# A post-norm attention and FFN block on one core: attention rows turned and normalised in the attention stage instead of the FFN stage

## The chip, the cores and the metric

The kernel runs on one core of a Trainium2 chip. The metric is the device time of one launch in microseconds (us), the median of several runs. TensorE (PE) multiplies into PSUM, which has eight banks of 512 fp32 columns; VectorE (DVE), ScalarE (ACT) and GpSimd (POOL) do the rest; SyncE (SP) only issues DMAs. Each engine runs its own instruction stream in order and waits on semaphores.

## The reference

The inputs are x of 4 x 2048 x 512 in fp32, four 512 x 512 weight matrices, a scale and a bias. There are 16 heads of 32 columns.

```python
q, k, v = x @ Wq.T, x @ Wk.T, x @ Wv.T           # split into 16 heads of 32
attn = softmax(q @ k.T / sqrt(32), axis=keys)
x = layernorm(x + attn @ v)                       # heads side by side: 512 columns
w = (weights >= 0) * 2 - 1
y = clip((x @ w.T) * scale + bias, -100, 100)
out = layernorm(x + y)
```

## The kernel before

Three stages follow one another, each a block of its own in which all engines start and end together.

**Projection** (`project`) makes q, k and v for 16 blocks of 512 tokens. Its products are full-array matmuls of 128 rows x 128 columns (L228). Once in each block, between two of them, stand eight matmuls that use 32 columns of the array each and four of which run side by side (L250).

**Attention** (`attend`) goes through 16 items (4 sequences x 4 groups of 4 heads), each with four query blocks of 512 queries (`qb`; 64 blocks in all, numbered `st`), each with 16 key tiles `kt` of 128 keys. For one key tile and two heads (a unit, two a tile) PE makes scores (L637, 8 matmuls, 32 array columns each, four side by side) into one of three PSUM slots; ACT takes the exponential of all 1024 columns of the unit (L780) into `probs`, a ring of eight tiles; PE multiplies them with v (L669, also on 32 array columns) into a bank that holds the block's output, with channels on the partitions and queries on the columns. PE's scores run `LAG` = 2 key tiles ahead of its values. A score unit waits for the exponential of three units earlier, the values of a tile for both exponentials of the tile.

The softmax denominators are sums over all keys. DVE adds `probs` of neighbouring tiles in five groups (`EDGES`) into `total` and `partial`; POOL issues DMAs that add the `partial` groups onto `total`. When block `st` is past, the work that is left of it is done between the key tiles of block `st`+1:

- DVE copies the block's output from its bank to SBUF after tile 2 (`copy_out`, L809), and SP stores it to DRAM, channel-major.
- PE sums `total` over its partitions with a matrix of ones (`denominators`, L690), 128 queries at a time, behind tiles 8, 10, 12 and 13 (`DEN_TILES`), again on 32 array columns a head. The denominators stand replicated over the 32 channels of a head.
- DVE copies them after tile 13 (`copy_den`, L814), and SP stores one row for each head.

**Normalise and FFN** (`normalise_and_ffn`) goes through 64 tiles of 128 tokens. It is a software pipeline written out by hand: in step `j` each engine does its part for tiles that entered at different times (`ATTN, LN1, TRANS, FFN, CLIP, LN2 = 0, 1, 2, 4, 5, 6` steps back). In one step:

- PE: four transposes of the attention tile into token-major order (L1003) and one of the denominators (L1004); four transposes of the first layernorm's result y (L1010); the bias row (L1017) and twelve matmuls of the FFN (L1021).
- DVE: clip (L1108), statistics of the two layernorms (L1084), reciprocal of the denominators (L1115), aggregation (L1089), the product of attention and reciprocal (L1122), reciprocal deviations (L1094), offsets (L1098), the low half of y's transposes (L1132).
- ACT: two square roots (L1035), the high half of y's transposes (L1055), the first layernorm's result y (L1039), then the second's.
- POOL: the two residual additions (L978, L985). SP loads attention, denominators and x for four tiles at a time.

Of the kernel before, what the change touches and what calls it, by code (L numbers as in the profile page):

```python
# [26 lines left out]
P = 128  # L27
# [30 lines left out]
DEN_TILES = (8, 10, 12, 13)  # L58
DEN_EDGES = (0, 128, 256, 384, BLK)
OUT_AFTER = 2  # L60
DEN_AFTER = 13
# [345 lines left out]
def attend(nc, ctx, dram, banks, ffn, first, early):  # L407
# [18 lines left out]
    ones = sb("ones", [P, HD], FP32)  # L426
# [7 lines left out]
    out_sb, den_sb = wf_scaled[:, 0:2, :], wf_scaled[:, 2:4, :]  # L434
# [11 lines left out]
    a_out = sem("a_out")  # L446
    a_dout = sem("a_dout")
    a_store = [sem(f"a_store{h}") for h in range(2)]
# [15 lines left out]
    HEAD = DEN_TILES[-1] + 1  # L464
# [8 lines left out]
    def out_bank(qb):  # L473

        return 2 * SLOTS + qb % 2
# [8 lines left out]
    def _(sp):  # L484
        def store(it, qb):

            cols = slice(qb * BLK, (qb + 1) * BLK)
            sp.wait_ge(a_out, it * QB + qb + 1)
            dst = dram["attn"].rearrange("n (g p) t -> (n g) p t", p=P)[bass.ds(it, 1), :, cols]
            sp.dma_start(dst.rearrange("o p t -> (o p) t"), out_sb[:, qb % 2, :]).then_inc(a_store[qb % 2], 16)  # L490
            sp.wait_ge(a_dout, it * QB + qb + 1 + 2)
            dst = dram["den"].rearrange("(i h) t -> i h t", h=G)[bass.ds(it, 1), :, cols]
            sp.dma_start(dst.rearrange("o h t -> (o h) t"), den_sb[0:P:HD, qb % 2, :]).then_inc(a_store[qb % 2], 16)

        def finish_stores():
            for h in range(2):
                sp.wait_ge(a_store[h], (LAST * QB // 2) * 32 + 32)
            attn_first, den_first, first_in = first
            sp.dma_start(attn_first[:], dram["attn"][0, :, 0:BLK].rearrange("(c p) t -> p c t", p=P)).then_inc(first_in, 16)
            sp.wait_ge(a_const, 5)  # L500
            sp.dma_start(den_first[0:H, :], dram["den"][0:H, 0:BLK]).then_inc(first_in, 16)
# [82 lines left out]
        for h in range(2):  # L584
            sp.wait_ge(a_store[h], ITEMS * QB // 2 * 32 + 32)

    @block.gpsimd
    def _(pool):
        nc.gpsimd.memset(ones[:], 1.0).then_inc(a_const, 1)  # L589
# [5 lines left out]
        nc.gpsimd.memset(first[1][:], 0.0).then_inc(a_const, 4)  # L595
# [23 lines left out]
    def _(pe):  # L619
# [53 lines left out]

        def denominators(it, qb, piece):
            st = it * QB + qb
            cols = slice(DEN_EDGES[piece], DEN_EDGES[piece + 1])
            split = it is LAST and qb == QB - 1
            parts = [total[:, qb % 2], partial[:, GROUPS - 2]] if split else [total[:, qb % 2]]
            if piece == 0:
                for pair in range(2):  # L680
                    if split:
                        pe.wait_ge(a_merge[qb % 2][pair], merged_after(it, qb, MERGES - 1))
                        pe.wait_ge(a_sum[pair], (st + 1) * KT + P_RING)
                    else:
                        pe.wait_ge(a_merge[qb % 2][pair], merged_after(it, qb, MERGES))
                pe.wait_ge(a_out, st + 1)
            for part in parts:
                for h in range(G):
                    rows = slice(HD * h, HD * h + HD)
                    last = nc.tensor.matmul(banks[rows, out_bank(qb), cols], ones[:], part[:, h, cols],  # L690
                                            start=(part is parts[0]), stop=(part is parts[-1]))
            last.then_inc(a_den, 1)

        def steps(scores, it, phase, qb, tiles):

            for kt in tiles:
# [8 lines left out]

                if kt in DEN_TILES and qb > 0:
                    denominators(it, qb - 1, DEN_TILES.index(kt))
                elif kt in DEN_TILES and not (isinstance(it, int) and it == 0):
                    denominators(it - 1, QB - 1, DEN_TILES.index(kt))

        def item(scores, it, phase):
# [6 lines left out]
            else:  # L718
                for piece in range(len(DEN_TILES)):
                    denominators(it, QB - 1, piece)  # L720

# [14 lines left out]
        with pe.If(needed < 1):  # L736
            pe.wait_ge(a_const, 1)
# [3 lines left out]
        with pe.Else():  # L741
            pe.wait_ge(a_const, 1)
# [22 lines left out]

# [21 lines left out]
    def _(dve):  # L787
        for pair in range(2):
            dve.sem_inc(a_sum[pair], P_RING)
        dve.sem_inc(a_store[0], 32)  # L790
        dve.sem_inc(a_store[1], 32)
# [14 lines left out]
        def copy_out(st, parity):  # L806
            dve.wait_ge(a_pv, st * KT + KT + P_RING)
            dve.wait_ge(a_store[parity], (st - parity) * 16 + 32)
            nc.vector.tensor_copy(out_sb[:, parity, :], banks[:, out_bank(parity), :]).then_inc(a_out, 1)  # L809

        def copy_den(st, parity):
            dve.wait_ge(a_den, (st + 1 + 2) * len(DEN_TILES))
            dve.wait_ge(a_store[parity], (st - parity) * 16 + 32)
            nc.vector.tensor_copy(den_sb[:, parity, :], banks[:, out_bank(parity), :]).then_inc(a_dout, 1)  # L814

        def item(it, first):
            for qb in range(QB):
                st = it * QB + qb
                for kt in range(KT):
                    if kt in EDGES:  # L820
                        continue
# [14 lines left out]
                    if kt == OUT_AFTER and not (first and qb == 0):  # L836
                        copy_out(st - 1, (qb - 1) % 2)
                    if kt == DEN_AFTER and not (first and qb == 0):
                        copy_den(st - 1, (qb - 1) % 2)
# [3 lines left out]
        copy_out(ITEMS * QB - 1, 1)  # L843
        copy_den(ITEMS * QB - 1, 1)


def normalise_and_ffn(nc, ctx, dram, x, ffn, first, banks, out):
# [16 lines left out]
    attnT = [first[0], sb("attnT1", [P, DC, BLK], FP32)]  # L864
    den_in = [first[1], sb("den_in1", [P, BLK], FP32)]
    rden = sb("rden", [P, 2, H], FP32)
    attn = sb("attn", [P, 2, D], FP32)
# [15 lines left out]
    f_den = sem("f_den")  # L883
    f_in = [first[2], sem("f_in1")]
    f_x = [sem(f"f_x{k}") for k in range(2)]
    f_aT = sem("f_aT")
    f_rden = sem("f_rden")
    f_attn = sem("f_attn")
# [12 lines left out]

    def aT_bank(s):
        return banks[:, s % 2, :]

    def den_bank(s):
        return banks[:, 6 + s % 2, 0:H]
# [32 lines left out]
    def _(sp):  # L939
# [3 lines left out]
        def load(b, batch, column, k):  # L943

            sp.wait_ge(f_res[0], b * TPB + TPB)
            src = dram["attn"][bass.ds(batch, 1), :, bass.ds(column, BLK)]
            sp.dma_start(attnT[k][:], src.rearrange("o (c p) t -> p (o c) t", p=P)).then_inc(f_in[k], 16)
            src = dram["den"].rearrange("(n h) t -> n h t", n=N)[bass.ds(batch, 1), :, bass.ds(column, BLK)]
            sp.dma_start(den_in[k][0:H, :], src.rearrange("o h t -> (o h) t")).then_inc(f_in[k], 16)
# [3 lines left out]
        sp.wait_ge(f_den, 1)  # L953
# [9 lines left out]
    def _(pool):  # L963
        nc.gpsimd.memset(ident3[:], 0.0).then_inc(f_const, 1)
        nc.gpsimd.memset(eps[:], EPS).then_inc(f_const, 1)
        nc.gpsimd.memset(den_in[1][:], 0.0).then_inc(f_den, 1)
# [6 lines left out]
        def step(r, j):  # L973
# [6 lines left out]
            if t is not None:  # L980
                if s % TPB == 0:
                    pool.wait_ge(f_x[s // TPB], r * 16 + 16)
                pool.wait_ge(f_attn, t + 1 + 2)
                pool.wait_ge(f_y[0], t + 1)
                nc.gpsimd.tensor_tensor(res1[:, s % 2], attn[:, s % 2], x_in[:, s // TPB, s % TPB], ALU.add).then_inc(f_res[0], 1)  # L985
# [4 lines left out]
    def _(pe):  # L990
# [3 lines left out]
        def step(r, j):  # L994
            t, s = tile(r, j, ATTN)
            if t is not None:
                k = s // TPB
                cols = slice(s % TPB * P, (s % TPB + 1) * P)
                if s % TPB == 0:
                    pe.wait_ge(f_in[k], r * 32 + 32)  # L1000
                pe.wait_ge(f_attn, t + 1)
# [71 lines left out]
    def _(dve):  # L1073
        dve.sem_inc(f_attn, 2)
# [26 lines left out]
        def step(r, j):  # L1101
# [9 lines left out]
            attn_t, attn_s = tile(r, j, ATTN)  # L1111
            if attn_t is not None:
# [117 lines left out]
```

## Time and profile before

| | us |
|---|---|
| median of 3 runs (2723.27 to 2724.31) | 2723.47 |
| the profiled execution, its own time | 2722.63 |
| its span from the first to the last instruction | 2720.5 |
| projection, until the first scores | about 560 |
| attention | about 1878 |
| normalise and FFN | about 282 |

The rows of the trace give for each engine when an instruction or a run of like instructions starts and how long it is busy. A PE matmul's duration includes its way through the array, so rows of neighbouring matmuls overlap: the work that one puts on PE is the distance between starts. A busy share of 100% on PE therefore doesn't say that PE has no time left.

### The profile page before, as it was taken

What the parts mean: (1) busy time and instruction counts of PE and PEld (TensorE: products, weight loads), DVE (VectorE), ACT (ScalarE), POOL (GpSimd) and SP (SyncE); (2) the same over time, 40 slices, a digit from 0 to 9 for tenths busy, and PEclk for the clock granted to TensorE, in tenths of its full rate; (3) what the DMA queues carried; (4) which work ended last, traced back from release to release, by engine and by line L of the source; (5) the groups of instructions that cost most, each with busy time, mean ns of one, the idle gap of its engine ahead of it and who ended that gap; (6) DMA issues with size and microseconds to landing.
All of it is one profiled execution on the core that took longest, in us unless ns stands there. A gap on an engine that the chain in (4) does not pass through costs nothing.

```text
span 2720.5 us, 92280 instructions
## 1 busy us (share of the span) xinstructions
PE 2685.3 (99%) x38720; PEld 1581.4 (58%) x38720; DVE 2193.1 (81%) x2623; ACT 2260.5 (83%) x2726; POOL 615.2 (23%) x661
## 2 busy tenths in 40 slices
PE   9999999999999999999999999999999999979998
PEld 8888888744454444444444444445455544447887
DVE  7444444379989989989989989989998998978998
ACT  5333333399999999999999999999999999965665
POOL 1000000012222222222222222222222222225665
PEclk9999999999999999999999999999999999989999
DMA  6555555589898999989899898999989899975553
GB/s 230 191 195 193 186 186 186 197 170 199 172 208 176 200 188 193 202 168 210 172 199 194 179 207 175 199 184 199 194 173 206 177 201 187 184 178 176 190 189 136
DMA packets 262711, 513.33 MB, mean 189 GB/s; under 512 B 20674, under 2 KB 135362, under 8 KB 260164
## 3 DMA queue, kind: packets, MB, share of 16 engines
q0 software_dynamic: 73440, 267.42, 52.4%
q1 hardware_dynamic: 179108, 222.61, 25.4%
q10 hardware_dynamic: 9792, 17.83, 1.7%
q8 instruction: 297, 4.87, 0.7%
q14 instruction: 74, 0.61, 0.1%
HBM read 122.43 MB, written 117.96 MB: 88 GB/s over the span
## 4 chain that ended last, share of the span: by engine, by line
PE 97%; DVE 1%; ACT 1%; issue 1%; DMA 0%; SPq 0%; POOL 0%; ACTq 0%; POOLq 0%; DVEq 0%
PE banks L637 34%; PE banks L669 33%; PE banks L228 19%; PE banks L1021 7%; PE banks L690 2%; PE banks L1010 1%; PE banks L1003 1%; PE banks L1017 1%; PE banks L250 0%; PE banks L1004 0%; PE banks L256 0%; DMA scratch_v<-v_out 0%; DMA score_rows<-scratch_k_lo 0%; ACT y L1039 0%; DVE qk_raw L357 0%
## 5 line engine op out<-in xcount | busy, mean ns | idle before, releaser
L780 ACT ACTIVATE probs<-banks 128x1024 f32<-128x1024 f32 x2048 | 1877.5, 1781 | 4.1 <-PE banks L637 4.1
L637 PE MATMUL banks<-score_rows 97*32 97x512 f16 x16384 | 1259.4, 382 | 4.9 <-POOL den_in L595 3.9
L669 PE MATMUL banks<-probs,v_keys 128*32 128x256 f32 x16384 | 1251.6, 379 | 0.5 <-ACT probs L780 0.5
L609 POOL DMA_DIRECT2D total<-partial x510 | 439.0, 861 | 1439.2 <-DVE partial L835 498.6
L835 DVE TENSOR_TENSOR partial<-partial,probs 128x1024 f32<-128x1024 f32 x640 | 748.4, 1221 | 0.0
L669 PEld LDWEIGHTS banks<-probs,v_keys 128*32 128x32 f32 x16384 | 510.5, 110 | 405.8 <-ACT probs L780 0.9
L831 DVE TENSOR_TENSOR partial<-probs 128x1024 f32<-128x1024 f32 x512 | 604.2, 1222 | 119.9 <-issue 109.7
L637 PEld LDWEIGHTS banks<-score_rows 97*32 97x32 f16 x16384 | 351.4, 95 | 509.7 <-ACT probs L780 413.2
L356 DVE TENSOR_TENSOR qk_lo<-banks,qk_hi 128x512 f16<-128x512 f32 x128 | 88.4, 691 | 241.7 <-ACT qk_hi L311 241.6
L311 ACT ACTIVATE qk_hi<-banks 128x512 f16<-128x512 f32 x128 | 76.0, 594 | 185.2 <-PE banks L228 185.2
L228 PE MATMUL banks<-xT_hi,w_hi 128*128 128x512 f32 x512 | 197.6, 390 | 0.0
L228 PE MATMUL banks<-xT_lo,w_hi 128*128 128x512 f32 x512 | 197.5, 389 | 0.0
L228 PE MATMUL banks<-xT_hi,w_lo 128*128 128x512 f32 x512 | 197.4, 389 | 0.0
L831 DVE TENSOR_TENSOR total<-probs 128x1024 f32<-128x1024 f32 x128 | 150.9, 1222 | 6.7 <-ACT probs L780 6.3
L835 DVE TENSOR_TENSOR total<-total,probs 128x1024 f32<-128x1024 f32 x128 | 151.0, 1223 | 0.0
L315 ACT ACTIVATE v_out<-banks 128x512 f32<-128x512 f32 x64 | 38.2, 597 | 123.9 <-PE banks L228 123.8
L589 POOL MEMSET ones<- 128x32 f32 x1 | 0.1, 124 | 501.4 <-POOLq L1190 501.4
L1035 ACT ACTIVATE std<-mean_var,eps 128x1 f32<-128x1 f32 x128 | 31.8, 289 | 97.8 <-DVE mean_var L1089 97.5
L228 PEld LDWEIGHTS banks<-xT_hi,w_lo 128*128 128x128 f32 x512 | 96.2, 188 | 19.9
L228 PEld LDWEIGHTS banks<-xT_lo,w_hi 128*128 128x128 f32 x512 | 96.2, 188 | 19.9
L228 PEld LDWEIGHTS banks<-xT_hi,w_hi 128*128 128x128 f32 x512 | 96.1, 188 | 19.8
L690 PE MATMUL banks<-total,ones 128*32 128x128 f32 x2048 | 101.8, 273 | 4.4 <-DVE wf_scaled L809 3.7
(95 smaller groups left out, 2180.4 us busy)
## 6 DMA issues: line engine op xcount, KB each, us to landing
total<-partial POOLq DMA_DIRECT2D x510, 512.0 KB, 6.2
scratch_q_raw<-qk_raw SPq DMA_DIRECT2D x16, 1024.0 KB, 5.7
scratch_k_raw<-qk_raw SPq DMA_DIRECT2D x16, 1024.0 KB, 5.7
scratch_v<-v_out SPq DMA_DIRECT2D x16, 1024.0 KB, 5.1
score_rows<-scratch_q_hi SPq DMA_DIRECT2D x128, 128.0 KB, 5.5
score_rows<-scratch_k_hi SPq DMA_DIRECT2D x128, 128.0 KB, 4.3
v_keys<-scratch_v SPq DMA_DIRECT2D x64, 256.0 KB, 7.0
scratch_attn<-wf_scaled SPq DMA_DIRECT2D x64, 256.0 KB
```

The costliest lines, as they stand in the source:

```text
L228: last = nc.tensor.matmul(bank(j), *parts[i], start=(c == 0 and i == 0), stop=(c == DC - 1 and i == 2))
L311: nc.scalar.activation(qk_hi[:, j, :], bank(j), ACT.Copy).then_inc(s_hi, 1)
L315: nc.scalar.activation(v_out[:, j - NQK, :], bank(j), ACT.Copy).then_inc(s_hi, 1)
L356: nc.vector.tensor_tensor(qk_lo[:, j, :], bank(j), qk_hi[:, j, :], ALU.subtract).then_inc(s_lo, 1)
L609: pool.dma_start(total[:, qb % 2, heads], partial[:, g - 1, heads], accum_op=ALU.add).then_inc(a_merge[qb % 2][pair], 16)
L637: last = nc.tensor.matmul(scores_of(phase, unit)[part, i, :], k_rows[:, h, keys], q_rows[:, h, qb * BLK:(qb + 1) * BLK], start=True, stop= ...
L669: last = nc.tensor.matmul(banks[rows, out_bank(qb), cols], v_keys[:, kt, rows], probs[:, kt % P_RING, h, cols], start=(kt == 0 and part == ...
L690: last = nc.tensor.matmul(banks[rows, out_bank(qb), cols], ones[:], part[:, h, cols], start=(part is parts[0]), stop=(part is parts[-1]))
L780: nc.scalar.activation(probs[:, kt % P_RING, heads, :], scores_of(it % SLOTS, qb * UNITS + u), ACT.Exp, scale=SCALE / GAIN ** 2).then_inc( ...
L831: nc.vector.tensor_tensor(into, probs[:, (kt - 1) % P_RING, heads], probs[:, kt % P_RING, heads], ALU.add).then_inc(a_sum[pair], 2)
L835: nc.vector.tensor_tensor(into, into, probs[:, kt % P_RING, heads], ALU.add).then_inc(a_sum[pair], 1)
L1021: last = nc.tensor.matmul(ffn_bank(s), part[:, s % 4, cols], w[:, c, :], start=False, stop=(c == DC - 1 and w is wf_lo))
```

## The change

The output of a query block and its denominators are now transposed on PE inside the next query block, divided there by DVE, and stored as normalised rows, token-major: `scratch_attn` becomes 4 sequences x 4 head groups x 2048 tokens x 128 channels. The FFN stage loads these rows and adds x to them; its five transposes a tile of L1003 and L1004, its reciprocal L1115 and its product L1122 are gone. Behind the key tiles of block `st`+1 there is now:

- after tile 2, DVE `copy_out` as before, into one buffer instead of two;
- behind tile 4, PE `turn_output`: four transposes of 128 x 128, the whole array, into the bank from which the output was just copied; after tile 5, DVE `copy_turned` to SBUF;
- behind tiles 8, 9, 10 and 11 the denominators, with `select` (a column of ones, a different one for each 128 queries) in the place of `ones`, so that the four pieces add up in the same 128 columns;
- at tile 12, DVE `copy_den` of these 128 columns; behind tile 13, PE `turn_denominators`, one transpose; after tile 14, DVE `invert_den` (16 values a partition); at tile 15, DVE `normalise` (512 columns, SBUF to SBUF).

SP waits for `a_norm` and issues one store of 256 KB a block in rows of 512 bytes, in the place of one of 2 KB rows and one of the denominators. In the FFN stage the attention rows of four tiles come in four DMAs.

```diff
-DEN_TILES = (8, 10, 12, 13)
+DEN_TILES = (8, 9, 10, 11)
+TURN_TILE = 4
+DEN_TURN_TILE = 13
+OUT_AFTER, TURNED_AFTER, DEN_AFTER, INVERT_AFTER, NORMAL_AFTER = 2, 5, 12, 14, 15
...
+        def turn_output(it, qb):
+            st = it * QB + qb
+            pe.wait_ge(a_out, st + 1)
+            for c in range(TPB):
+                cols = slice(c * P, (c + 1) * P)
+                last = nc.tensor.transpose(banks[:, out_bank(qb), cols], out_sb[:, cols], ident2[:])
+            last.then_inc(a_turn, 1)
...
-                pe.wait_ge(a_out, st + 1)
+                pe.wait_ge(a_turned, st + 1)
...
-                    last = nc.tensor.matmul(banks[rows, out_bank(qb), cols], ones[:], part[:, h, cols],
+                    last = nc.tensor.matmul(banks[rows, out_bank(qb), 0:P], select[:, piece, :], part[:, h, cols],
...
+        def turn_denominators(it, qb):
+            pe.wait_ge(a_dcopy, it * QB + qb + 1)
+            nc.tensor.transpose(banks[:, out_bank(qb), P:2 * P], den_sb[:], ident2[:]).then_inc(a_dturn, 1)
...
+        def copy_turned(st, parity):
+            dve.wait_ge(a_turn, st + 1)
+            dve.wait_ge(a_norm, st)
+            nc.vector.tensor_copy(turned, banks[:, out_bank(parity), :]).then_inc(a_turned, 1)
...
+        def invert_den(st, parity):
+            dve.wait_ge(a_dturn, st + 1)
...
+        def normalise(st, parity):
+            dve.wait_ge(a_dout, st + 1 + 2)
...
 def normalise_and_ffn(nc, ctx, dram, x, ffn, first, banks, out):
...
-                for c in range(DC):
-                    nc.tensor.transpose(aT_bank(s)[:, c * P:(c + 1) * P], attnT[k][:, c, cols], ident3[:])
-                nc.tensor.transpose(banks[:, 6 + s % 2, 0:P], den_in[k][:, cols], ident3[:]).then_inc(f_aT, 1)
...
-                nc.vector.reciprocal(rden[:, attn_s % 2], den_bank(attn_s)).then_inc(f_rden, 1)
...
-                nc.vector.tensor_tensor(attn[:, attn_s % 2].rearrange("p (h d) -> p h d", h=H),
-                                        aT_bank(attn_s).rearrange("p (h d) -> p h d", h=H),
-                                        rden[:, attn_s % 2].unsqueeze(2).to_broadcast([P, H, HD]), ALU.mult).then_inc(f_attn, 1)
```

PE in one query block of attention, before, from the last values of key tile 8 to the first of tile 10 (`probs,v_keys` are values, `score_rows` scores, `total,ones` denominators; 32x marks the array columns used):

```order
L669 MATMUL banks<-probs,v_keys 32x256 x4
L690 MATMUL banks<-total,ones 32x128 x4
L637 MATMUL banks<-score_rows 32x512 x8
L669 MATMUL banks<-probs,v_keys 32x256 x4
L637 MATMUL banks<-score_rows 32x512 x8
L669 MATMUL banks<-probs,v_keys 32x256 x4
L637 MATMUL banks<-score_rows 32x512 x8
L669 MATMUL banks<-probs,v_keys 32x256 x4
```

PE in the same block now, around tile 4, and then around tile 13 (`ident,wf_scaled` are the transposes of the output, `ident,den_sb` that of the denominators; 128x is the whole array):

```order
L642 MATMUL banks<-score_rows 32x512 x8
L674 MATMUL banks<-probs,v_keys 32x256 x4
L685 MATMUL banks<-ident,wf_scaled 128x128 x4
L642 MATMUL banks<-score_rows 32x512 x8
L674 MATMUL banks<-probs,v_keys 32x256 x4
```

```order
L642 MATMUL banks<-score_rows 32x512 x8
L674 MATMUL banks<-probs,v_keys 32x256 x4
L713 MATMUL banks<-ident,den_sb 128x128
L642 MATMUL banks<-score_rows 32x512 x8
L674 MATMUL banks<-probs,v_keys 32x256 x4
```

Before, every matmul of the attention stage stood on 32 array columns; now two places in each block have the whole array between them.

PE in one step of the FFN stage before, from the last FFN matmul of the step ahead:

```order
L1021 MATMUL banks<-wf_lo,yT_hi 128x512
L1003 MATMUL banks<-ident,attnT 128x128 x4
L1004 MATMUL banks<-ident,den_in 128x128
L1010 MATMUL banks<-ident,y 128x128 x4
L1017 MATMUL banks<-bias_rows,bias_ones 128x512
L1021 MATMUL banks<-wf_hi,yT_hi 128x512
```

The same place now:

```order
L1063 MATMUL banks<-wf_lo,yT_hi 128x512
L1052 MATMUL banks<-ident,y 128x128 x4
L1059 MATMUL banks<-bias_rows,bias_ones 128x512
L1063 MATMUL banks<-wf_hi,yT_hi 128x512
```

The transposes of y now follow directly on the FFN matmuls of the step ahead.

## Rows read from the trace of the kernel before

**Rows 1.** The page, its first line

```profile
span 2720.5 us, 92280 instructions
```

**Rows 2.** Groups by line: busy us, mean ns of one, idle before

```profile
L780 ACT ACTIVATE probs<-banks 128x1024 f32<-128x1024 f32 x2048 | 1877.5, 1781 | 4.1 <-PE banks L637 4.1
```

**Rows 3.** Windows: each engine's busy us, granted PE clock, DMA share, GB/s

```profile
1000.00:1500.00 500.00, 500.00 (x9276) 240.30 (x9272) 452.52 (x411) 500.00 (x547) 116.73 (x136) 1.00 0.93 192
...
2600.00:2650.00 50.00, 50.00 (x274) 41.95 (x273) 48.29 (x154) 31.04 (x64) 31.98 (x26) 1.00 0.58 196
```

**Rows 4.** Timeline of PE in attention: start us, busy us, engine, line

```profile
1213.40 0.39 PE L690 MATMUL banks<-total,ones 128*32 128x128 f32 x8
1213.61 0.61 PE L637 MATMUL banks<-score_rows 97*32 97x512 f16 x8
...
1214.48 0.61 PE L637 MATMUL banks<-score_rows 97*32 97x512 f16 x8
...
1229.02 0.61 PE L637 MATMUL banks<-score_rows 97*32 97x512 f16 x8
...
1229.94 0.61 PE L637 MATMUL banks<-score_rows 97*32 97x512 f16 x8
```

**Rows 5.** Waits over the whole run: us in total, times, longest

```profile
PEld banks L637 <- ACT probs L780: 413.2, 1410, 0.8
```

**Rows 6.** Timeline of PE in the projection, where the array is divided

```profile
101.57 0.39 PE L228 MATMUL banks<-w_hi,xT_lo 128*128 128x512 f32 x1
101.89 0.61 PE L250 MATMUL banks<-squares,head_sum 128*32 128x512 bf16 x8
102.43 0.50 PE L228 MATMUL banks<-w_hi,xT_hi 128*128 128x512 f32 x1
102.77 0.39 PE L228 MATMUL banks<-w_lo,xT_hi 128*128 128x512 f32 x1
```

**Rows 7.** Timeline of PE in one FFN step

```profile
2602.18 0.60 PE L1003 MATMUL banks<-ident,attnT 128*128 128x128 f32 x4
...
2602.72 0.60 PE L1010 MATMUL banks<-ident,y 128*128 128x128 f32 x4
...
2603.08 0.48 PE L1017 MATMUL banks<-bias_rows,bias_ones 128*128 128x512 f32 x1
...
2605.96 0.40 PE L1021 MATMUL banks<-wf_lo,yT_hi 128*128 128x512 f32 x1
...
2606.20 0.60 PE L1003 MATMUL banks<-ident,attnT 128*128 128x128 f32 x4
```

**Rows 8.** Timeline of DVE and ACT in the same FFN step

```profile
2602.47 0.69 DVE L1108 TENSOR_SCALAR clipped<-banks 128x512 f32<-128x512 f32 x1 [0.23 <-PE banks L1021]
...
2603.07 1.27 DVE L1084 BATCH_NORM_STATS2 stats<-res 128x6 f32<-128x512 f32 x2
...
2604.27 0.24 DVE L1115 RECIPROCAL rden<-banks 128x16 f32<-128x16 f32 x1
...
2604.43 0.26 DVE L1089 BATCH_NORM_AGGREGATE mean_var<-stats 128x2 f32<-128x6 f32 x2
...
2604.58 0.48 ACT L1035 ACTIVATE std<-mean_var,eps 128x1 f32<-128x1 f32 x2 [1.51 <-DVE mean_var L1089]
2604.63 0.69 DVE L1122 TENSOR_TENSOR attn<-banks,rden 128x512 f32<-128x512 f32 x1
...
2604.97 0.58 ACT L1055 ACTIVATE yT_hi<-banks 128x512 fp32r<-128x512 f32 x1
...
2605.68 1.52 ACT L1039 ACTIVATE y<-res,offset,rstd 128x512 f32<-128x512 f32 x2
```

**Rows 9.** Timeline of DVE in attention, the denominators' copy

```profile
1223.19 0.69 DVE L814 COPY wf_scaled<-banks 128x512 f32<-128x512 f32 x1 [0.94 <-PE banks L690]
```

**Rows 10.** Timeline from the end of attention into the FFN stage

```profile
2434.66 0.69 DVE L814 COPY wf_scaled<-banks 128x512 f32<-128x512 f32 x1 [2.97 <-PE banks L690]
...
2438.27 0.39 SPq L941 DMA_DIRECT2D x_res<-in_x  x1
```

More of the change, by code:

```diff
@@ L485, in store @@
         def store(it, qb):
[L487 to L493, printed above, removed]
+            sp.wait_ge(a_norm, it * QB + qb + 1)
+            dst = dram["attn"].rearrange("n g (b c q) f -> (n g) b q c f", b=QB, q=P)[bass.ds(it, 1), qb]
+            src = normal[:, qb % 2, :].rearrange("q (c f) -> q c f", c=TPB)
+            sp.dma_start(dst.rearrange("o q c f -> (o q) c f"), src).then_inc(a_store[qb % 2], 16)
         def finish_stores():
             for h in range(2):
[L497 to L501, printed above, removed]
+                sp.wait_ge(a_store[h], (LAST * QB // 2) * 16 + 16)
+            attn_first, first_in = first
+            for t in range(TPB):
+                src = dram["attn"][0, :, t * P:(t + 1) * P, :].rearrange("g p f -> p g f")
+                sp.dma_start(attn_first[:, t].rearrange("p (g f) -> p g f", g=NG), src).then_inc(first_in, 16)
         sp.wait_ge(early.s_vst, 16 * NBLK)
@@ L689, in denominators, with behind @@
                     rows = slice(HD * h, HD * h + HD)
-                    last = nc.tensor.matmul(banks[rows, out_bank(qb), cols], ones[:], part[:, h, cols],
-                                            start=(part is parts[0]), stop=(part is parts[-1]))
+                    last = nc.tensor.matmul(banks[rows, out_bank(qb), 0:P], select[:, piece, :], part[:, h, cols],
+                                            start=(piece == 0 and part is parts[0]),
+                                            stop=(piece == TPB - 1 and part is parts[-1]), skip_group_check=True)
             last.then_inc(a_den, 1)
+        def turn_denominators(it, qb):
+            pe.wait_ge(a_dcopy, it * QB + qb + 1)
+            nc.tensor.transpose(banks[:, out_bank(qb), P:2 * P], den_sb[:], ident2[:]).then_inc(a_dturn, 1)
+        def behind(it, qb, kt):
+            if kt == TURN_TILE:
+                turn_output(it, qb)
+            if kt in DEN_TILES:
+                denominators(it, qb, DEN_TILES.index(kt))
+            if kt == DEN_TURN_TILE:
+                turn_denominators(it, qb)
         def steps(scores, it, phase, qb, tiles):
@@ L704, in steps @@
                     values(it, qb, kt, half)
[L706 to L709, printed above, removed]
+                if qb > 0:
+                    behind(it, qb - 1, kt)
+                elif kt < HEAD and not (isinstance(it, int) and it == 0):
+                    behind(it - 1, QB - 1, kt)
         def item(scores, it, phase):
@@ L718, in item @@
             else:
-                for piece in range(len(DEN_TILES)):
+                turn_output(it, QB - 1)
+                for piece in range(TPB):
                     denominators(it, QB - 1, piece)
+                turn_denominators(it, QB - 1)
         def all_items(scores):
@@ L818, in item, with finish_last @@
                 st = it * QB + qb
+                def finish_last(kt):
+                    if first and qb == 0:
+                        return
+                    if kt == OUT_AFTER:
+                        copy_out(st - 1, (qb - 1) % 2)
+                    if kt == TURNED_AFTER:
+                        copy_turned(st - 1, (qb - 1) % 2)
+                    if kt == DEN_AFTER:
+                        copy_den(st - 1, (qb - 1) % 2)
+                    if kt == INVERT_AFTER:
+                        invert_den(st - 1, (qb - 1) % 2)
+                    if kt == NORMAL_AFTER:
+                        normalise(st - 1, (qb - 1) % 2)
                 for kt in range(KT):
                     if kt in EDGES:
+                        finish_last(kt)
                         continue
@@ L835, in item @@
                             nc.vector.tensor_tensor(into, into, probs[:, kt % P_RING, heads], ALU.add).then_inc(a_sum[pair], 1)
[L836 to L839, printed above, removed]
+                    finish_last(kt)
         for it in range(ITEMS):
```

103 lines of the change are left out of this document (45 added, 58 removed).

## The prediction, made before the changed kernel ran

> **What bounds the kernel now.** The time divides at the stage borders, and each stage has its own limit, so I read the windows of one stage first and then the timeline inside it. In attention (the window from 1000) [rows 3] PE and ACT both show 500 of 500 us, DVE 452.5. Which of the two sets the pace is told by the other views. ACT takes 1877.5 us for 2048 units, 0.917 us each [rows 2], with next to no idle time. PE's busy share hides waits: its weight loads waited 1410 times for ACT, 413 us in total [rows 5], and the starts of score groups come in two rhythms [rows 4]: 0.92 us when PE waits for ACT (1229.02 to 1229.94) and 0.87 us when it catches up after a denominators' piece (1213.61 to 1214.48). So ACT is the bound of attention, 32 x 0.917 = 29.34 us a query block, and PE follows closely. How closely is the number on which the case turns.
>
> PE's own demand: from 1213.61 to 1229.02 lie 17 units and three pieces of denominators of 0.21 us each (1213.40 to 1213.61 is one) [rows 4]. (15.41 - 0.64) / 17 = 0.869 us a unit. A block needs 32 x 0.869 + 4 x 0.21 = 28.65 us. **PE has 0.69 us to spare in each block of 29.34.**
>
> In the FFN stage the reader is to see a period of 4.02 us a tile on PE, from one group of L1003 to the next, without a gap [rows 7], and DVE with 48.29 of 50 us just beneath it [rows 3].
>
> **What the FFN stage loses.** The five transposes take 2602.72 - 2602.18 = 0.54 us [rows 7], 0.107 each; what is left of the step is 4.02 - 0.54 = 3.48. If PE stayed the bound, 64 tiles would give 34 us. It doesn't stay: with the attention transposes gone, PE's first work in a step is the transposes of y, and y comes late. I follow the loop. DVE's clip starts 0.20 to 0.29 us after PE's last matmul has streamed (2602.18 to 2602.47 is the 0.29). From the clip to the start of y on ACT lie 2605.68 - 2602.47 = 3.21 us [rows 8]. Of these the reciprocal took 0.16 (2604.27 to 2604.43); the 0.61 of L1122 lay beside ACT's square roots and isn't won, since the second aggregation still has to wait for its statistics and ACT has roots and yT_hi ahead of y. I take 3.03 (bounds 2.92 and 3.05), and y takes 0.81, so y is there 3.84 us after the clip. PE then needs 0.04 us of handing over and 3.48 of work until the clip after the next can start, 0.24 later. y of step j is transposed in step j+1, so this loop spans two steps: (3.84 + 0.04 + 3.48 + 0.24) / 2 = 3.80 us a step. Before, the 0.54 us of L1003 and L1004 stood at the head of the step and covered this wait. DVE's and ACT's own round (clip 0.6, statistics 1.2, aggregation to yT_hi about 0.65, yT_hi 0.58, yT_lo 0.6) comes to some 3.65 us, under it. Gain: 0.22 us x 64 tiles = **-14 us**, bounds -8 and -34. The four loads of attention rows instead of two are hidden: a block of four tiles lasts 15 us.
>
> **What the attention stage gets, PE.** The same five transposes, 0.54 us a block. The denominators cost what they did: 4 pieces x 16 matmul records, only earlier. To the 0.54 comes what no row of attention shows: these are the only matmuls there on the whole array. The nearest rows are in the projection, where eight matmuls on 32 columns stand between full ones [rows 6]. From the last full matmul before (101.57) to the second after (102.77) pass 1.20 us. The work in it is 0.23 + 0.43 + 0.23 = 0.89 (full matmuls follow one another at 0.23; eight of 512 columns side by side in fours take 0.43, as a score group does). **0.31 us is lost for one excursion**, at both edges together: the array runs empty, and the next weights aren't loaded beneath the running matmuls (the weights of L228 start with its matmul). The rows show the reverse nesting, narrow inside wide, but both have one edge of each kind. A block now has two excursions, at tiles 4 and 13: 0.62 us. PE's demand is 28.65 + 0.54 + 0.62 = 29.81, against ACT's 29.34. PE becomes the bound by 0.47 us a block, in 63 blocks 30 us, less the head start of some 1 us that the three slots hold: **+29 us**. Bounds: 0 if the excursions are hidden (29.19 stays under 29.34); +41 if each costs 0.40, which is what the fp32 weight loads add if none overlaps.
>
> The Trainium skill, TensorEngine Tiling (Array Packing), section Tiling Modes, has the rule for this: changing the tiling mode, not merely the tile, drains TensorE. The trace agrees in that the 0.31 us stands only where the number of active columns changes. It gives no price; by the rule with a free drain the stage would stay at ACT's pace, which is the third rival below.
>
> **DVE in attention.** Before 0.69 x 2 for the copies; now 0.69 x 2 (output and its transposes), 0.69 for the product (as L1122 [rows 8]), 0.24 for the reciprocal (as L1115) and about 0.3 for 128 columns: 2.6 us, 1.2 more a block. DVE is busy 452.5 of 500 us, 26.55 of 29.34 [rows 3], and 0.94 us of its idle time is the wait for the last denominators between two additions of the last group [rows 9]; the new place of this copy, between two groups, lies in slack. 27.8 of 29.3 fits, and fits better if PE stretches the block. PE's new waits queue scores behind them: for `copy_out` at tile 4, where DVE is some 2 us ahead, for `copy_turned` at tile 8 and for `copy_den` at tile 13, both further ahead. ACT has no instruction more; POOL's merges are untouched. SP waits up to four units longer in `store`; behind it stand loads of q and v for the next item, needed more than 10 us later. The store of 256 KB has four times the packets on DMA engines that are busy 0.93 [rows 3]; nothing waits for it.
>
> **The border of the stages.** After the last block the chain is longer by the transposes, two copies for one, a transpose and reciprocal, the product: 0.4 + 0.7 + 0.1 + 0.25 + 0.7, less 0.4 for the smaller copy, and five handovers of 0.2 to 0.3. That delays the last store by 3 to 5 us; the store of 2.9 us behind it (2435.35 to 2438.27 [rows 10]) and x's load follow as before. **+4 us.**
>
> **Sum.** The profiled execution took 2722.63 us, with a span of 2720.5 [rows 1], 0.8 us under the median of 2723.47. 2722.6 + 29 - 14 + 4 = 2741.6 us.
>
> **The rivals.**
> 1. The forecast: PE bounds attention, y's loop bounds the FFN stage; 2741.6, own range 2729 to 2752.
> 2. PE stays the bound of the FFN stage (y is ready earlier than I think, by 0.6 us): 34 us gained, 2722.6 + 29 - 33 + 4 = 2723, no change. For it: the busy sum of no other engine is over 3.2 us a step. Against: the order of ACT's queue.
> 3. The excursions are hidden or cheap, and attention stays at ACT's pace; faster. Threshold: 0.075 us an excursion, (0.69 - 0.54) / 2. 2722.6 - 14 + 4 = 2713, with rival 2 on top 2694. For it: PE's weight loads wait for ACT 0.29 us at a time (413.2 / 1410 [rows 5]), so the price might fall into waits. Against: the waits add up to 0.69 us a block only, and 0.54 is already spent on the transposes.
> 4. DVE or the DMAs bind too: late copies make PE wait at tiles 4 or 13 with scores queued behind, 0.2 us or more a block; 2753 and up.
>
> **How the numbers follow.** Chances: forecast 0.53, rival 2 0.15, rival 3 0.22, rival 4 0.10. A measurement here tells about 0.2%, 5.4 us, from no change. Slower: forecast and rival 4, 0.62 or a little more; same: rival 2 and the costlier side of rival 3, 0.17; faster: 0.20. The range leaves out half of rival 4 and the lower end of rival 3: 2706 to 2752.
>
> **What the profile after would show.** In attention, PE's weight loads of scores hardly wait for ACT any more, ACT gets idle time in small pieces of 0.47 us a block in all, and blocks last 29.8 us; around the transposes, starts are 0.1 us wider than the work. In the FFN stage, PE waits for y each second step or in each, with steps of 3.8 us. Wrong would be a block of 29.34 with PE still waiting (rival 3), a step of 3.48 (rival 2), or PE waiting for DVE in attention (rival 4).

## The result, and the profile after

The changed kernel takes 2738.98 us, median of 5 runs (2738.05 to 2739.43), against 2723.27 before: a ratio of 1.0058 with a 95% interval of 1.0045 to 1.0072, so 15.7 us slower. 2741.6 was predicted. The profiled execution has a span of 2736.6 us, 16.1 more than [rows 1].

The page and the waits of the kernel after, the lines that answer to [rows 2] and [rows 5]:

```profile
span 2736.6 us, 92216 instructions
...
L812 ACT ACTIVATE probs<-banks 128x1024 f32<-128x1024 f32 x2048 | 1896.7, 1073 | 11.7 <-PE banks L642 5.4
```

```profile
PEld banks L713 <- issue: 25.9, 63, 0.4
PEld banks L685 <- issue: 25.9, 63, 0.4
PEld banks L642 <- ACT probs L812: 17.4, 83, 0.4
```

PE's weight loads of scores used to wait 413.2 us for the exponentials, 1410 times; now it is 17.4 us, 83 times. (Weight loads run ahead of the matmuls, so these waits are no measure of PE's spare time: 413.2 us would be 6.5 us a block, and PE had 0.69.) PE has nothing left to wait for: it has become the bound of the attention stage. The other two lines are the first weight load of each whole-array place. The weight loads pause there for 0.41 us, 63 times each: these weights are not loaded beneath the matmuls ahead. ACT doesn't show its new idle time as such. Before, a record lasted 1781 ns at a distance of 917 from one start to the next, so neighbours overlapped by 0.86 us; now it is 1073 ns at 930, and they overlap by 0.14. The busy sum is even larger than before. The reader should take the bound from who waits, not from the busy sums.

The timeline of PE around the two whole-array places of one block (start us, busy us, engine, line), kernel after, which answers to [rows 4] and [rows 6]:

```profile
1202.38 0.65 PE L642 MATMUL banks<-score_rows 97*32 97x512 f16 x8
1202.82 0.65 PE L674 MATMUL banks<-probs,v_keys 128*32 128x256 f32 x8
1203.40 0.33 PE L713 MATMUL banks<-ident,den_sb 128*128 128x128 f32 x1
1203.66 0.62 PE L642 MATMUL banks<-score_rows 97*32 97x512 f16 x8
...
1215.37 0.60 PE L674 MATMUL banks<-probs,v_keys 128*32 128x256 f32 x8
1215.90 0.66 PE L685 MATMUL banks<-ident,wf_scaled 128*128 128x128 f32 x4
1216.49 0.61 PE L642 MATMUL banks<-score_rows 97*32 97x512 f16 x8
```

One group of values, or of scores, lasts 0.434 us up to the next start, half of a unit of 0.868 (1202.38 to 1202.82 is one of scores). From the values at 1202.82 to the scores at 1203.66 pass 0.84 us: 0.434 of values, 0.107 for the one transpose, and **0.30 us for leaving the 32-column layout and coming back**. At the four transposes it is 1216.49 - 1215.37 = 1.12, less 0.434 and 0.43: 0.26 us. The predicted price was 0.31, read from the projection.

How long a block is now, by the denominators' copy on DVE in two blocks that follow one another, kernel after, which answers to [rows 9]:

```profile
1200.05 0.29 DVE L851 COPY den_sb<-banks 128x128 f32<-128x128 f32 x1 [1.40 <-PE banks L705]
...
1229.80 0.29 DVE L851 COPY den_sb<-banks 128x128 f32<-128x128 f32 x1 [1.40 <-PE banks L705]
```

29.75 us, against 29.33 before (29.34 from ACT's sum) and 29.81 predicted. DVE waits for PE here, 1.40 us, and not the other way round.

The FFN stage, timeline of the kernel after (which answers to [rows 7] and [rows 8]):

```profile
2620.49 0.69 DVE L1149 TENSOR_SCALAR clipped<-banks 128x512 f32<-128x512 f32 x1
...
2620.61 0.66 PE L1052 MATMUL banks<-ident,y 128*128 128x128 f32 x4 [0.15 <-ACT y L1081]
...
2623.43 1.52 ACT L1081 ACTIVATE y<-res,offset,rstd 128x512 f32<-128x512 f32 x2
...
2624.37 0.65 PE L1052 MATMUL banks<-ident,y 128*128 128x128 f32 x4
2624.43 0.69 DVE L1149 TENSOR_SCALAR clipped<-banks 128x512 f32<-128x512 f32 x1 [0.19 <-PE banks L1063]
...
2628.11 0.69 DVE L1149 TENSOR_SCALAR clipped<-banks 128x512 f32<-128x512 f32 x1
...
2628.24 0.66 PE L1052 MATMUL banks<-ident,y 128*128 128x128 f32 x4 [0.17 <-ACT y L1081]
```

Steps of 3.76 and 3.87 us, 3.78 in the mean between 2500 and 2700 us (4.02 before, 3.80 predicted). PE waits for y in each second step, by 0.15 to 0.20 us as a rule, which it hardly did before, because the attention transposes stood in front. The clip too waits for PE in each second step, by 0.1 to 0.2 us, and not in the others. That is y's loop over two steps: transposes of y at 2620.61, clip at 2624.43 (3.82 us later), y at 2627.37 (2.94 later, as from 2620.49 to 2623.43; 3.21 before), transposes at 2628.24 (0.87 later), 7.63 us for two steps. It lies just above the round of DVE and ACT (2624.43 to 2628.11, 3.68 us without a wait).

The three shares, between marks that both traces have: first to last exponential 1877.5 us before, 1904.3 after (+26.8); from there to the first bias row of the FFN 29.9 and 33.8 (+3.9); from there to the end 263.5 and 249.0 (-14.5). The sum is +16.2. The first share is the surest. Where the other two divide isn't sharp, because around the border the granted clock is at its lower level (0.50 from 2440 to 2460 us before, from 2470 to 2490 after). How long it stays there once the FFN has begun differs from profile to profile: the first step between bias rows takes 5.44 us in the kernel before and 4.01 in the kernel with one unneeded transpose below, which has the same FFN stage. Border and FFN stage together are steadier: 293.4 and 292.8 us in these two, 282.8 to 284.3 in three kernels with the new attention stage and the FFN stage of the kernel after. The change takes about 10 us there.

### The profile page after: what moved, and what is told of

Read it like the earlier page. It is cut to its first block and busy times, and to the rows that moved or that the text cites. A ratio compares the mean times of both kernels' runs of the same rounds, so it can differ in the third digit from the quotient of the medians.

```text
span 2736.6 us, 92216 instructions
## 1 busy us (share of the span) xinstructions
PE 2690.3 (98%) x38720; PEld 1722.2 (63%) x38720; DVE 2214.1 (81%) x2687; ACT 2277.5 (83%) x2726; POOL 613.0 (22%) x663
## 5 line engine op out<-in xcount | busy, mean ns | idle before, releaser
L812 ACT ACTIVATE probs<-banks 128x1024 f32<-128x1024 f32 x2048 | 1896.7, 1073 | 11.7 <-PE banks L642 5.4
L674 PE MATMUL banks<-probs,v_keys 128*32 128x256 f32 x16384 | 1268.4, 379 | 0.0
L674 PEld LDWEIGHTS banks<-probs,v_keys 128*32 128x32 f32 x16384 | 539.6, 110 | 377.7 <-issue 0.9
L642 PEld LDWEIGHTS banks<-score_rows 97*32 97x32 f16 x16384 | 463.2, 96 | 344.5 <-ACT probs L812 17.4
L705 PE MATMUL banks<-total,select 128*32 128x128 f32 x2048 | 108.8, 274 | 0.9 <-DVE wf_scaled L846 0.9
```

The costliest lines, as they stand in the source:

```text
L642: last = nc.tensor.matmul(scores_of(phase, unit)[part, i, :], k_rows[:, h, keys], q_rows[:, h, qb * BLK:(qb + 1) * BLK], start=True, stop= ...
L674: last = nc.tensor.matmul(banks[rows, out_bank(qb), cols], v_keys[:, kt, rows], probs[:, kt % P_RING, h, cols], start=(kt == 0 and part == ...
L705: last = nc.tensor.matmul(banks[rows, out_bank(qb), 0:P], select[:, piece, :], part[:, h, cols], start=(piece == 0 and part is parts[0]), ...
L812: nc.scalar.activation(probs[:, kt % P_RING, heads, :], scores_of(it % SLOTS, qb * UNITS + u), ACT.Exp, scale=SCALE / GAIN ** 2).then_inc( ...
```

## The experiments

Four kernels change the kernel after, and four change the kernel before; two put together what the first ones gave. Ratios are to the kernel before, which ran beside each of them at 2723.2 to 2723.3 us.

**The same work on 32 columns.** The transposes of attention are replaced by matmuls that keep PE as long without touching the whole array (the transposing itself is left out, so the rows stored aren't the attention rows):

```diff
-                last = nc.tensor.transpose(banks[:, out_bank(qb), cols], out_sb[:, cols], ident2[:])
+                for h in range(G):      # for two of the four column groups: 8 matmuls, 0.43 us
+                    rows = slice(HD * h, HD * h + HD)
+                    last = nc.tensor.matmul(banks[rows, out_bank(qb), cols], out_sb[:, rows], ident2[:], start=True, stop=True)
...
-            nc.tensor.transpose(banks[:, out_bank(qb), P:2 * P], den_sb[:], ident2[:]).then_inc(a_dturn, 1)
+            for h in range(G):
+                rows = slice(HD * h, HD * h + HD)
+                last = nc.tensor.matmul(banks[rows, out_bank(qb), P:P + P // 2], den_sb[:, rows], ident2[:, 0:P // 2],
+                                        start=True, stop=True)
+            last.then_inc(a_dturn, 1)
```

> The changed kernel with each full-array transpose in attention replaced by fp32 matmuls on 32 array columns that keep PE as long (eight for the four transposes, 0.43 us; four of 64 columns for the single one, 0.107 us). It leaves the transposing out, so its rows are not the attention rows. Theory (the loss is the change between 32 columns and the whole array, about 0.28 us an excursion): PE's demand falls from 29.75 to about 29.2 us a block, under ACT's 29.34, and some 26 us come back: 2713. Rival (the transposes' work itself, or DVE's and SP's part of the change, holds the block at 29.75): it stays at 2739.

Measured: 2714.21 us (2712.32 to 2715.66), a ratio of 0.9967 (0.9954 to 0.9979), 25 us under the kernel after. The waits of this kernel show PE with time to spare again:

```profile
PEld banks L642 <- ACT probs L818: 133.8, 511, 0.4
```

Blocks last 29.33 us. The work that the change adds to PE fits into its spare time; what doesn't fit is the change of layout. The edit also puts plain matmuls in the place of transposes, but that isn't what is paid for: in the projection [rows 6] plain matmuls stand on both sides, and the price is the same 0.31 us. All other parts of the change in attention (DVE's five operations in the place of two, the store, the waits) are in this kernel and cost next to nothing (attention lasts 1878.8 us, against 1877.5 before).

**No transposes at all.** Both calls become a `sem_inc`; the transposing is left out here too.

> The changed kernel without any of the five transposes of a block in attention; DVE's copies, reciprocal and product and all waits stay. It leaves the transposing out. Theory: nothing more is to be had than in the run with the same work on 32 columns, since ACT bounds both: 2713, blocks of 29.34 us, less up to 2 us in the last block's chain. Rival (the work of the transposes counts too): clearly under that run, by 0.54 us a block or a part of it, up to 34 us.

Measured: 2711.18 us (2709.39 to 2712.23), ratio 0.9953 (0.9936 to 0.9969). 3 us under the run before, of which the last block's chain can explain up to 2 (from the last exponential to the first bias row 31.7 us, against 33.4), and not the 34 us that the work would be if it counted. ACT bounds both.

**The denominators turned on 32 columns.** Only 16 columns of that transpose are used, so four matmuls can make them in the 32-column layout:

```diff
-            nc.tensor.transpose(banks[:, out_bank(qb), P:2 * P], den_sb[:], ident2[:]).then_inc(a_dturn, 1)
+            pick = ident2[:].rearrange("p (h r) -> p h r", h=G)[:, :, 0:TPB]
+            for j in range(G):
+                rows = slice(HD * j, HD * j + HD)
+                last = nc.tensor.matmul(banks[rows, out_bank(qb), P:P + G * TPB], den_sb[:, rows], pick, start=True, stop=True)
+            last.then_inc(a_dturn, 1)
```

> The changed kernel computing everything, with the denominators turned by four matmuls of 32 array columns that give only the 16 columns used, in the place of the full transpose: one excursion a block instead of two. Theory: a block loses 0.41 us (0.107 of work, 0.30 of excursion) and gets back up to 0.1, so 29.40 to 29.45 against 29.75: about 20 us faster, 2719. Rival (an excursion costs nothing by itself): 0 to 3 us faster.

Measured: 2724.24 us (2721.72 to 2725.38), ratio 1.0002 (0.9992 to 1.0011): 15 us faster than the kernel after, and no different from before. The timeline of PE of this kernel, the output's transposes in two blocks that follow one another, and the place of the new turn:

```profile
1210.40 0.66 PE L685 MATMUL banks<-ident,wf_scaled 128*128 128x128 f32 x4
...
1227.07 0.65 PE L674 MATMUL banks<-probs,v_keys 128*32 128x256 f32 x8
1227.50 0.23 PE L716 MATMUL banks<-ident,den_sb 128*32 128x16 f32 x5
1227.56 0.38 PE L642 MATMUL banks<-score_rows 97*32 97x512 f16 x1
1227.57 0.20 PE L716 MATMUL banks<-ident,den_sb 128*32 128x16 f32 x3
1227.60 0.61 PE L642 MATMUL banks<-score_rows 97*32 97x512 f16 x7
1227.99 0.65 PE L674 MATMUL banks<-probs,v_keys 128*32 128x256 f32 x8
```

The turn costs 0.05 us (1227.07 to 1227.99, less two groups of 0.434) in the place of 0.41. A block lasts 29.50 us, though, not 29.40 to 29.45. Laid beside the kernel after, unit by unit (medians over the blocks), some 0.1 us comes back in two places. The twelve units between the turn and the output's transposes take 0.871 us each in the place of 0.867, together 0.05 us. And from the scores ahead of the output's transposes to those behind them pass 1.61 us in the place of 1.555, so this one excursion costs 0.31 us here and 0.26 there. Why PE is slower in these units, these runs don't tell. It isn't for want of a whole-array place: where PE catches up, the kernel before and the one with the same work on 32 columns have 0.867 to 0.869 and no such place in the stage.

**y's transposes later in the FFN step.**

```diff
+                for c in range(DC):
+                    if c == 1:
+                        turn()          # the wait for y and its four transposes, which stood ahead of the bias row
```

> The changed kernel with PE's order in an FFN step altered: bias row and the first three FFN matmuls (0.93 us) ahead of y's transposes, the other nine behind them. Theory (y's loop over two steps makes the step 3.76 us): PE no longer waits for y, and the next bound is the round of DVE and ACT, 3.67 us from clip to clip as the steps without a wait on PE show: 0.09 us x 64, about 6 us faster, 2733. Rival (PE's own work with gaps makes the step): no change. Rival (the round of DVE and ACT isn't a bound): steps of 3.48, 18 us faster.

Measured: 2728.59 us (2727.02 to 2730.0), ratio 1.0021 (1.0011 to 1.003), 10 us faster than the kernel after. The mean step is 3.66 us: PE's wait is gone, no clip waits for PE any more between 2500 and 2700 us, and the round of DVE and ACT stands next, as expected. The second to the fifth step, before this round is felt, take 3.45 to 3.47 us: PE's own pace, predicted at 3.48. In the profiles the stretch from the first bias row on gives 6.6 us of the gain, attention 1.3, which the edit doesn't touch, and the border 2.5. These 2.5 us belong to the edit, which moves the first bias row:

```profile
2483.79 0.78 PE L1063 MATMUL banks<-bias_rows,bias_ones 128*128 128x512 f32 x1
...
2485.66 1.11 PE L1053 MATMUL banks<-ident,y 128*128 128x128 f32 x4
```

It now stands ahead of the third tile's transposes, where in the kernel after it is behind them (transposes at 2486.88, bias row at 2487.65). So the edit is worth some 9 us, where 6 were expected.

**The spare time of the kernel before, measured by whole-array transposes that are not needed.** Ahead of the first, of two, or of all four pieces of denominators, one transpose of the identity into columns that the piece then overwrites:

```diff
+            if piece in (0,):            # (0, 2) and (0, 1, 2, 3) in the other two
+                nc.tensor.transpose(banks[:, out_bank(qb), cols], ident2[:], ident2[:])
```

> The kernel before with one more full-array transpose of the identity in each block, ahead of the first piece of denominators (its result is overwritten, so everything is still computed). Theory: 0.107 us of work and 0.30 of excursion raise PE's demand from 28.65 to 29.06 us a block, still under ACT's 29.34: no change, 0 to 1 us. Rival (PE has no spare time and every us added counts): 0.41 x 63, 26 us slower.

> As the run with one such transpose, but two, ahead of the first and third piece. Theory: demand 28.65 + 0.82 = 29.47 us, over ACT's 29.34 by 0.13, up to 0.25 with the slower rhythm of 0.871 us a unit that the run with the narrow turn of the denominators shows: 8 to 16 us slower, where one cost nothing. Rival (an excursion costs only its work): demand 28.86, no change.

> As before, but four, one ahead of each piece. Theory: demand 28.65 + 1.64 = 30.29 us, 0.95 over ACT: 60 us slower. Rival (only the work): demand 29.08, no change.

Measured: one, 2723.86 us, ratio 1.0004 (0.9994 to 1.0013); two, 2732.44, 1.0037 (1.0023 to 1.0051), 9 us; four, 2781.98, 1.0216 (1.0199 to 1.0233), 59 us. Blocks last 29.33, 29.44 and 30.23 to 30.25 us. The timeline of PE with four, one excursion, and the same place of the next block:

```profile
1204.10 0.33 PE L688 MATMUL banks<-ident 128*128 128x128 f32 x1
1204.36 0.42 PE L692 MATMUL banks<-total,ones 128*32 128x128 f32 x8
...
1233.79 0.61 PE L669 MATMUL banks<-probs,v_keys 128*32 128x256 f32 x8
1234.33 0.33 PE L688 MATMUL banks<-ident 128*128 128x128 f32 x1
1234.59 0.42 PE L692 MATMUL banks<-total,ones 128*32 128x128 f32 x8
1234.83 0.62 PE L637 MATMUL banks<-score_rows 97*32 97x512 f16 x8
```

From the values to the scores 1.04 us, less 0.434, 0.107 and 0.21: 0.29 for the excursion. By the sum (28.65 plus 0.40 each) the three should be 29.34, 29.45 and 30.25 us, and they are. The price is nothing as long as the total stays under ACT's 29.34 us, and all of it from there on.

**Four times the same work on 32 columns, in the kernel before.**

```diff
+            if piece in (0, 1, 2, 3):
+                half = slice(cols.start, cols.start + P // 2)
+                for h in range(G):
+                    rows = slice(HD * h, HD * h + HD)
+                    nc.tensor.matmul(banks[rows, out_bank(qb), half], ident2[:, rows], ident2[:, 0:P // 2], start=True, stop=True)
```

> The kernel before with the same work in the same four places but on 32 array columns: four matmuls of 64 columns each, 0.107 us a place. Theory: demand 28.65 + 0.43 = 29.08 us, under 29.34: no change, 0 to 1 us, where four on the whole array cost 60. Rival (added instructions as such, or a stall of the first piece, cost the time): as much as the run with four wide ones.

Measured: 2729.95 us (2727.16 to 2731.44), ratio 1.0024 (1.0014 to 1.0033): 6.6 us slower, where 0 to 1 were expected, though far from the 59 of the wide ones. The timeline of PE shows both what was right and what was missed, an ordinary block first:

```profile
1216.92 0.28 PE L691 MATMUL banks<-ident 128*32 128x64 f32 x8
...
1246.25 0.28 PE L691 MATMUL banks<-ident 128*32 128x64 f32 x8
...
1632.99 0.45 PE L691 MATMUL banks<-ident 128*32 128x64 f32 x6
1634.20 0.22 PE L691 MATMUL banks<-ident 128*32 128x64 f32 x1 [0.76 <-issue]
```

An ordinary block lasts 29.33 us. Nine of the 63, from one denominators' copy to the next, last 0.35 to 1.33 us longer, most of them with a pause of PE like the one at 1634.20, for which the trace names no cause. Attention as a whole takes 6.6 us more than before. In attention the profile has ten pauses of PE of this kind, 5.1 us in all. The smaller spare time alone doesn't explain the loss: the kernel with one wide transpose has about as little to spare (0.28 us a block, against 0.26), shows two such pauses, and its attention takes 0.6 us more than before. The kernel before has three, of 0.3 to 0.5 us, and loses nothing by them. So both count, that there are more pauses and that little is left to cover them. What makes them, and why this kernel has more, stays open.

**Both mendings together.**

> The changed kernel with both mended: the denominators turned on 32 columns, and y's transposes behind the first three FFN matmuls. Theory: the two gains lie in different stages and add up: 2724.2 less the 7 to 10 us that the later transposes gave, about 2716, steps of 3.66 us. Rival (one takes from the other): over 2720.

Measured: 2713.87 us (2712.35 to 2714.13), ratio 0.9965 (0.9952 to 0.9978): **25 us faster than the kernel after and 9 us faster than the kernel before**, and it computes everything; 2716 was expected. Blocks last 29.50 us, as with the narrow turn alone. The timeline of PE's bias rows shows the steps of 3.65 and 3.67 us:

```profile
2608.34 0.39 PE L1067 MATMUL banks<-bias_rows,bias_ones 128*128 128x512 f32 x1
...
2611.99 0.39 PE L1067 MATMUL banks<-bias_rows,bias_ones 128*128 128x512 f32 x1
...
2615.66 0.39 PE L1067 MATMUL banks<-bias_rows,bias_ones 128*128 128x512 f32 x1
```

**The round of DVE and ACT shortened as well.** On top of both, ACT makes yT_hi ahead of the square roots, and DVE makes yT_lo ahead of the reciprocal deviations.

```diff
 ACT: + yT_hi(TRANS)   deviation(LN1)   deviation(LN2)   - yT_hi(TRANS)   layernorm(LN1)   layernorm(LN2)
 DVE: clip   statistics   aggregate   + yT_lo(TRANS)   reciprocal_std   offset_of   - yT_lo(TRANS)
```

> As the run with both, and the round of DVE and ACT in an FFN step shortened: ACT makes the high half of y's transposes ahead of the two square roots, and DVE makes the low half between aggregation and reciprocal deviations, where the product stood before, so that it lies beside the square roots. Theory (after y's loop the round of DVE and ACT is the bound, 3.66 us): it falls to some 3.2 us, PE's own 3.48 becomes the step, 0.18 x 64 = 11 us faster than the run with both, about 2705. Rival (the step is held by something else, POOL's two additions of 2.6 us or y arriving later): steps of 3.6 or more, 2713 to 2716.

Measured: 2727.79 us (2723.99 to 2729.57), ratio 1.0016 (1.0007 to 1.0025): 14 us slower than without this reordering, and the mean step is 3.85 us between 2500 and 2700 us. The timeline of ACT, DVE and PE's transposes in this kernel, one round from one yT_hi to the next:

```profile
2612.97 0.60 ACT L1101 ACTIVATE yT_hi<-banks 128x512 fp32r<-128x512 f32 x1 [0.98 <-PE banks L1057]
2613.46 0.47 ACT L1087 ACTIVATE std<-mean_var,eps 128x1 f32<-128x1 f32 x2
2613.60 0.69 DVE L1167 TENSOR_TENSOR yT_lo<-banks,yT_hi 128x512 fp32r<-128x512 f32 x1 [0.53 <-ACT yT_hi L1101]
...
2614.20 0.21 DVE L1145 RECIPROCAL rstd<-std 128x1 f32<-128x1 f32 x2
2614.39 0.33 DVE L1149 TENSOR_SCALAR offset<-mean_var,rstd 128x1 f32<-128x1 f32 x2
2614.64 1.52 ACT L1091 ACTIVATE y<-res,offset,rstd 128x512 f32<-128x512 f32 x2 [0.71 <-DVE offset L1149]
...
2615.51 0.66 PE L1057 MATMUL banks<-ident,y 128*128 128x128 f32 x4 [0.50 <-ACT y L1091]
...
2616.33 0.34 ACTq L1118 DMA_DIRECT2D out_x<-y  x1
...
2616.78 0.60 ACT L1101 ACTIVATE yT_hi<-banks 128x512 fp32r<-128x512 f32 x1 [0.62 <-PE banks L1057]
```

The new bound is a loop of DVE and ACT that closes in one step, 3.81 us here. yT_lo waits for yT_hi; the reciprocals and offsets now stand behind yT_lo; ACT's two layernorms wait for the offsets, 0.71 us; behind them ACT issues the store of the output (2616.33); and only then comes the next yT_hi. The profile puts the wait before yT_hi down to PE's transposes, but these had ended at 2616.17, 0.6 us earlier, while yT_hi starts 0.1 us behind the end of the store's issue, in this step and in most others (0.5 us in each eighth). In the kernels without the reordering this issue lay in ACT's wait for the statistics, beside which it cost nothing. The rival of the expectation held: y arrives later. I had added up each engine's own instructions and not followed this loop.

## Why the prediction was right

**The bound of attention.** ACT's 0.917 us a unit and PE's 28.65 us a block were right. That the spare time was 0.69 us, no more, is shown by the kernels with one, two and four excursions: the first free, the second at a part of its price, the others at the full one.

**The price of an excursion.** Predicted 0.31 us from the projection's rows, measured 0.26 to 0.31 in attention. That this term, and not the work, decides is shown by the run with the same work on 32 columns, which returns 25 us. Rival 3 (excursions hidden) and rival 4 (DVE or DMAs bind) fell. The Trainium skill, TensorEngine Tiling (Array Packing), section Tiling Modes, says that changing the tiling mode drains TensorE. The runs agree that such a change costs time, and give the size. How the 0.26 to 0.31 us divide between running empty and the weight load that isn't hidden (0.41 us of pause in the weight loads), they don't show.

**Attention as a whole.** +29 us predicted, +26.8 measured: the block came out 0.06 us shorter, mostly from the cheaper excursion at the four transposes (0.26 us). The head start of 1 us that was taken off doesn't show: 0.41 us in 63 blocks are 26 us.

**The FFN stage.** -14 us predicted, -14.5 measured between the marks. The step of 3.78 us (3.80) comes from y's loop over two steps. The loop measures 7.63 us in the rows above, against 7.60: from PE's transposes to the clip 3.82, against 3.48 + 0.24, and from the clip to y 2.94, against 3.03. These two were off by 0.1 us in opposite directions, and that they cancel is luck. That the loop is what binds is shown by the later transposes: with y's transposes 0.93 us later in PE's order the steps fall to 3.66, the round of DVE and ACT, also as estimated (3.65). Rival 2 (PE stays the bound at 3.48) fell.

**The border.** +4 us predicted, +3.9 in this pair of profiles. That the two agree to a tenth is luck: in kernels with the same chain the distance is 33.4 to 34.2 us after the change (29.9, and 30.7 with one unneeded transpose, before it), and the clock at the border moves it too. What holds is border and FFN stage together, -10 us as predicted (-14 + 4).

**What was wrong in detail.** The prediction expected ACT to show idle time of 0.47 us a block. It doesn't: its busy sum grew, to within 7.6 us of the 1904.3 us from the first to the last exponential; the loss stands in the waits of PE, which vanish. It gave 16 matmul records for a piece of denominators, where the rows have 8 [rows 4]; the time of 0.21 us is right. It put PE's waits at 0.69 us a block, as an argument against rival 3, where its own [rows 5] give 6.5 us of waiting weight loads; the 0.69 is right as spare time, but comes from the rhythms. And its sign that starts would be 0.1 us wider than the work around the transposes doesn't fit its own price; it was 0.26 and 0.30. In the experiments three expectations were too good: the narrow turn (20 us expected, 15 measured: slower units and a dearer excursion at the output's transposes), the four narrow dummies (nothing expected, 6.6 us: more single pauses than in the other kernels) and the reordered FFN step (11 us faster expected, 14 slower, for a loop that wasn't followed).

## What to carry to other kernels

Before work is moved into a stage, read the spare time of each of its engines as a number a round: the rhythm in which it waits against the rhythm in which it catches up. Work was free here up to that number (but for single pauses, when little was left) and cost its full price beyond it, and to the price belongs the way into another layout of the array: where a stage runs on 32 columns, it can pay to put small work into 32 columns too, even if that takes more matmuls (15 us here). Where work leaves a stage, ask what it covered: here transposes in front of PE's step hid a result that came late, and moving the waiting instruction behind work that doesn't need it gave 10 us. Before instructions of one engine are reordered, follow each loop through all engines, the issue of DMAs included.

## What the runs showed of the hardware

An excursion of PE from 32-column matmuls to the whole array and back costs 0.26 to 0.31 us beyond its work, in attention at both places of the kernel after, with one transpose and with four, and in the kernels with unneeded transposes, and also in the projection, where the nesting is reversed. PE's catch-up rhythm for the same stream of scores and values is 0.867 to 0.869 us a unit in most places, but 0.871 in the twelve units behind the narrow turn (and in the three ahead of the denominators' turn); nothing in the traces names the cause. ACT's records of 1781 ns at a pitch of 917 get shorter, to 1073 ns, when the engine is starved a little, while its busy sum grows from 1877.5 to 1896.7 us. And the issue of a store by ACT (0.34 us) costs nothing where ACT would wait anyway, and lengthens the step where it stands in the loop.
